# GNN layer on one core: in the node stage, VectorE takes the first activation remainder between two halves of the centring, and ScalarE rounds the first activation right behind its gelu

## What is computed

```python
h = jnp.maximum(_layernorm(x), 0.0)
Q, K, V = h @ Wq, h @ Wk, h @ Wv              # 8 heads of 32
...                                            # softmax over the edges of each destination, sum of V
out = out.reshape(n, 256) @ Wo_w + Wo_b
out = _layernorm(h + out, ln1_g, ln1_b)
ffn = gelu(out @ ffn_w1 + ffn_b1) @ ffn_w2 + ffn_b2     # 256 -> 512 -> 256
out = _layernorm(out + ffn, ln2_g, ln2_b)
return x + out
```

## Time and profile before

| | |
|---|---|
| median of 3 runs | 1871.33 us (1869.89 to 1872.53) |
| profiled execution | 1869.43 us, its span 1867.7 us |
| TensorE matmul busy, share of the span | 90% |
| TensorE weight load busy | 76% |
| VectorE busy | 79% |
| ScalarE busy | 69% |
| GpSimd busy | 72% |

### The profile page before, as it was taken

One profiled execution on the slowest core, in us unless ns is written; L12 is line 12 of the kernel. 1 busy time (PEld: TensorE's weight loads), 2 busy tenths in 40 slices (PEclk: granted clock), 3 DMA queues, 4 the chain that ended last, 5 costly groups with the idle time before them and its releaser, 6 DMA issues.

```text
span 1867.7 us, 29784 instructions
## 1 busy us (share of the span) xinstructions
PE 1684.7 (90%) x9846; PEld 1411.2 (76%) x9846; DVE 1471.2 (79%) x4479; ACT 1288.1 (69%) x2340; POOL 1337.4 (72%) x1342
## 2 busy tenths in 40 slices
PE   0999999639961599999999999999999999999997
PEld 0677777418741488888888888888888888888887
DVE  3565665367732599999999999999999999999996
ACT  1677777302210688888888888888888888888884
POOL 7777774007772777877887787778778877877783
PEclk9999999859985799999999999999999999999999
DMA  3778887313434577777776777777777767776761
GB/s 104 238 258 267 267 262 221 122 57 97 136 105 148 106 167 170 168 170 170 165 172 167 175 158 174 167 170 168 169 170 167 171 166 174 158 175 166 172 132 57
DMA packets 132414, 309.41 MB, mean 166 GB/s; under 512 B 14022, under 2 KB 68214, under 8 KB 132260
## 3 DMA queue, kind: packets, MB, share of 16 engines
q0 software_dynamic: 42624, 139.33, 37.2%
q1 hardware_dynamic: 37492, 115.61, 18.3%
q10 hardware_dynamic: 52144, 52.56, 8.5%
HBM read 140.66 MB, written 118.20 MB: 139 GB/s over the span
## 4 chain that ended last, share of the span: by engine, by line
PE 66%; DMA 1%; DVE 1%; POOL 0%; ACT 0%; SPq 0%; issue 0%; DVEq 0%; POOLq 0%; ACTq 0%
PE d_F L991 30%; PE d_Y L1002 30%; PE d_T L978 5%; DMA d_fb_row<-in_fb 1%; DMA d_z<-agg_scratch 0%; PE d_Y L968 0%; ACT d_zn L903 0%; PE d_F L961 0%; SPq L727 0%; POOL d_zx_rstd L788 0%; POOL d_u L775 0%; POOL d_u L773 0%; ACT d_z L914 0%; DVE d_y_stats L847 0%; DVE d_zx_stats L860 0%
## 5 line engine op out<-in xcount | busy, mean ns | idle before, releaser
L1002 PE MATMUL d_Y<-d_w_hi,d_act_hi 128*128 128x256 f32 x1568 | 458.5, 292 | 0.0
L1002 PE MATMUL d_Y<-d_w_hi,d_act_lo 128*128 128x256 f32 x1568 | 441.8, 282 | 0.0
L1002 PE MATMUL d_Y<-d_w_lo,d_act_hi 128*128 128x256 f32 x1568 | 441.7, 282 | 0.0
L903 ACT ACTIVATE d_zn<-d_z,d_zx_nmr,d_zx_rstd 128x256 f32<-128x256 f32 x392 | 224.3, 596 | 149.1 <-POOL d_zx_nmr L791 149.1
L991 PE MATMUL d_F<-d_zt_hi,d_w_hi 128*128 128x512 f32 x784 | 321.5, 410 | 2.1 <-DVE d_zt_lo L823 1.4
L991 PE MATMUL d_F<-d_zt_hi,d_w_lo 128*128 128x512 f32 x784 | 310.2, 396 | 0.0
L991 PE MATMUL d_F<-d_zt_lo,d_w_hi 128*128 128x512 f32 x784 | 310.0, 395 | 0.0
L923 ACT ACTIVATE d_F<-d_F,d_fb_col 128x512 f32<-128x512 f32 x392 | 259.5, 662 | 61.5 <-PE d_F L991 61.4
L773 POOL TENSOR_TENSOR d_u<-d_zn,d_g_row 128x1024 f32<-128x1024 f32 x98 | 293.5, 2995 | 6.0 <-ACT d_zn L903 6.0
L1002 PEld LDWEIGHTS d_Y<-d_w_hi,d_act_lo 128*128 128x128 f32 x1568 | 296.1, 189 | 0.0
L1002 PEld LDWEIGHTS d_Y<-d_w_lo,d_act_hi 128*128 128x128 f32 x1568 | 295.9, 189 | 0.0
(11 more groups left out here) (159 smaller groups left out, 3538.5 us busy)
## 6 DMA issues: line engine op xcount, KB each, us to landing
agg_scratch<-a_bias_row ACTq DMA_DIRECT2D x50, 1024.0 KB, 6.7
d_x<-in_x SPq DMA_DIRECT2D x98, 512.0 KB, 4.1
d_z<-agg_scratch POOLq DMA_DIRECT2D x98, 512.0 KB, 5.6
d_x<-d_b_wide POOLq DMA_DIRECT2D x98, 512.0 KB, 7.5
out<-d_o SPq DMA_DIRECT2D x98, 512.0 KB, 2.9
c_cont<-cont_scratch SPq DMA_DIRECT2D x25, 256.0 KB, 3.4
a_xd<-in_x,a_idx POOLq DMA_INDIRECT x100, 2.8
a_xs<-in_x,a_idx POOLq DMA_INDIRECT x100, 4.7
```

What stands on the lines that cost most here:

```text
L903: ins = nc.scalar.activation(zn[gz % 2][:, j, :], z[gz % ZR][:, j, :], ACT.Identity, bias=zx_nmr[:, at % NR, 0, j:j + 1], scale=zx_rstd[:, ...
L1002: ins = nc.tensor.matmul(Y[s % 2][:, j, :], a[:, c, j * P:(j + 1) * P], w[:, c, :], start=False, stop=(c == KF - 1 and w is w2_lo), skip_g ...
```

## The change

On VectorE the centring of the four rows is cut in two calls: rows 0 and 1 are centred, then the remainder of block 0 is taken, then rows 2 and 3 are centred. On ScalarE `high_part(0)` stands directly behind `gelu(0)`; the normalisation of row 2 of the next group, which stood between them, comes behind both.

```diff
@@ VectorE @@
+                    def centre(rows):
+                        if there(y):
+                            dve.wait_ge(ymv_done, y + 1)
+                            for j in rows:
+                                nc.vector.scalar_tensor_tensor(Y[yr][:, j, :], Y[yr][:, j, :], y_mv[:, yr, j, 0:1],
+                                                               g2_row[:], ALU.subtract, ALU.mult).then_inc(centred, 1)
+
...
                         ins.then_inc(ymv_done, 1)
-                        dve.wait_ge(ymv_done, y + 1)
-                        for j in range(GT):
-                            nc.vector.scalar_tensor_tensor(Y[yr][:, j, :], Y[yr][:, j, :], y_mv[:, yr, j, 0:1],
-                                                           g2_row[:], ALU.subtract, ALU.mult).then_inc(centred, 1)
+                    centre((0, 1))
                     low_part(s, 0)
+                    centre((2, 3))
@@ ScalarE @@
                     norm_z((0, 1))
                     gelu(0)
+                    high_part(0)
                     norm_z((2,))
-                    high_part(0)
                     gelu(1)
```

## The result

The changed kernel takes 1889.06 us in the median, the kernel before 1870.87 us in the runs beside it: ratio 1.0097, 95% interval 1.0082 to 1.0112. The change makes it 0.97% slower, 18.2 us. (Two of the changed kernel's six executions took 3410 and 3970 us, for a reason that isn't known; the median and the ratio leave them out.) The profiled execution took 1889.43 us, with a span of 1887.2 us.

The account below looks back on a forecast made before the run. The bound was the loop of VectorE's chain and TensorE's second transposes. 92 full steps x 0.20 = +18.4 us, last five steps -0.9, net +17.5 on the 1871.3 us median: 1888.8 us, range 1878 to 1895.

Parts of the forecast that it names:

- The loop: VectorE's chain from statistics to zt remainder, 8.99 us, then TensorE's 3.54 us from the second transposes: 12.53 us a step.
- The cost of the wait: VectorE waits for `act_hi` of block 0 before its remainder: 0.18 us, lengthening its chain by 0.20 us a step.
- ScalarE's dependent pair: Block 0's gelu and rounding back to back: 0.70 us between starts, as block 2's; VectorE sees the end 0.03 us later.
- Block 3's wait: TensorE's wait for block 0's remainder, in front of block 3 of the first product: 0.17 us a step, forecast gone.
- The second transposes: TensorE's wait there for the remainder of zt's first half: grows by 0.37 us to some 0.55 us listed idle.
- ScalarE's 0.11 us: ScalarE's later work shifts by the longer gelu-rounding pair, 0.70 against 0.59 us; costed at nothing, being covered.
- the last steps: The stage's last five steps, where VectorE's chain is short: gain TensorE's 0.17 us each, 0.9 us at most.
- One sign: VectorE idle some 0.19 us in front of the first remainder, with ScalarE's `act_hi` as releaser.
- the first rival: TensorE's wait for block 0 was the bound: 0.17 us gained in 97 steps, 16.5 us, 1854.8 us; chance 0.05.

Follow-up runs that it names:

- ScalarE's part alone: Kernel before, with only ScalarE's `high_part(0)` moved directly behind `gelu(0)`; VectorE still centres all four rows first: 1872.31 us, ratio 1.0006.
- three and one: Changed kernel, but three rows centred ahead of the remainder of block 0 and one behind it: 1872.35 us, ratio 1.0006 to the kernel before.
- VectorE's part alone: Changed kernel with ScalarE's old order put back, so only VectorE's centring is split: 1922.11 us, ratio 1.0277.
- the last version: Changed kernel, three rows centred first, x's aggregations and second statistics pair behind first zt remainder, ScalarE's zt first-half rounding ahead of block 3's gelu: 1834.65 us.
- the kernel before with the late aggregations: Kernel before, with the four aggregations of x's statistics moved on VectorE behind the first remainder of zt: 1852.08 us, ratio 0.9897.
- the changed kernel with the late aggregations: Changed kernel, with the four aggregations of x's statistics moved on VectorE behind the first remainder of zt: 1863.48 us, ratio 0.9959.

## Why the prediction was right, step by step

- **The total**: 1888.8 us forecast, 1889.1 measured. The stage itself, from its first to its last statistics instruction, grew by 17.4 us for the 17.5 forecast. That the totals agree within 0.3 us is partly luck: the four executions spread over 2 us, and the start of the stage moves by more than that.
- **The loop** held. Five versions lie on one line, two more 0.02 us above it, and the two that change only what lies beside the loop (ScalarE's part alone, three and one) don't move the time.
- **The cost of the wait**: 2.72 us against a place at 2.54, 0.18, as forecast. The full steps grew from 12.525 to 12.72, 0.196 us for the 0.20 forecast; over 92 steps 18.0 us for the 18.4.
- **ScalarE's dependent pair** takes 1234.16 - 1233.46 = 0.70 us from start to start, as block 2's pair did, and the remainder starts 0.03 us behind its end.
- **Block 3's wait**: gone. **The second transposes**: 0.56 us of listed idle time for the 0.55 forecast.
- **ScalarE's 0.11 us**: covered in the full steps, as forecast. In the last steps it isn't quite. There the zt remainder starts 1825.17 - 1817.23 = 7.94 us behind the statistics instead of 7.84, for ScalarE is 0.10 later, and each of these four steps gains 0.09 us instead of the 0.17 that I put down as the most; the whole end gives some 0.6 us and not 0.9. With ScalarE's old order (VectorE's part alone) the same four steps take 12.15 us and gain the full 0.17, so it is ScalarE's new order that costs them. That is too small to matter.
- **One sign was forecast wrongly**: that VectorE would show some 0.19 us of listed idle time, with `act_hi` as the releaser. No such note stands in the timeline. The two centring records end at 1233.81 + 0.88 = 1234.69, for a record goes on for 0.48 us where the next instruction could start after 0.39, and so the visible gap is only 0.10 us. The wait has to be read from the starts. In the version with VectorE's part alone it is 0.54 us long, and 0.46 are listed.

The Trainium skill, Perfetto Trace Analysis, section Optimization Strategy, says to find the gaps of the engine one optimises for and to make what ends them come sooner. Taken for the first gap alone, as the first rival took it, that would have given 1854.8 us. The runs bear it out only where the loop goes through the gap: closing the one in front of block 3 gave nothing while the second stood (three and one), closing the second gave 18.6 us, and closing the first as well then gave 5.3 us more.

## What to carry to other kernels

Where a busy engine waits at several places in each step, follow the step back from the last wait: a wait that lies before it, on a stretch that runs beside another engine's unbroken chain, is slack, and removing it only makes the later wait longer. It becomes worth something once that chain is short enough. To move an instruction forward on the engine whose chain sets the step is free only if its input is there already when the engine reaches it; the cost is the engine's idle time, once for each step. The cheap gain was to move work that nobody waits for behind the instruction that the other engine waits for: 1% with one block moved, 1.9% with the order of three and one and the moves of the last version added.

## What the runs showed that was not expected

The profile's chain of work that ended last changes its face without a change of the cause. Its line for the changed kernel, for the kernel before, and for the kernel before with the late aggregations:

```profile
DVE 32%; PE 28%; ACT 7%; DMA 1%; issue 1%; POOL 1%; SPq 0%; DVEq 0%; POOLq 0%
```
```profile
PE 66%; DMA 1%; DVE 1%; POOL 0%; ACT 0%; SPq 0%; issue 0%; DVEq 0%; POOLq 0%; ACTq 0%
```
```profile
PE 65%; DMA 1%; DVE 1%; ACT 0%; POOL 0%; issue 0%; SPq 0%; DVEq 0%; ACTq 0%; POOLq 0%
```

The second reads like the third, although in the kernel before the loop through VectorE was in force as in the changed kernel. With 0.19 us of idle time or less in front of the second transposes the chain doesn't show the wait, and the matmuls read as busy through it; in the changed kernel with the late aggregations, at 22.8 us in 80 steps or 0.29 us, it does (VectorE 31%), and at 0.56 us too. A TensorE that reads as busy for 50.00 of 50 us can still be waiting 0.2 us in each step.
